# Taking the products of constants out of TensorE's foreseen waits in a four-layer cross-attention kernel

## What is computed

```python
# L0: one-head attention over a projected memory, a gate, an RMS norm
memory_proj = ctx @ W_mem.T;  attn = softmax(x @ memory_proj.T / 16)
c = attn @ memory_proj
x = rmsnorm(x + sigmoid(concat(x, c) @ W_gate.T + b_gate) * c) * norm_w
# L1: 16 heads of 64 over ctx with a mask, then a GELU feed-forward of width 1024
q = layernorm(x) @ Wq;  k, v = split(ctx @ Wkv)
x = x + tanh(attn_gate) * (softmax(mask(q @ k.T / 8)) @ v) @ Wo
x = x + tanh(ff_gate) * gelu(layernorm(x) @ W1) @ W2
# L2, L3: causal self-attention (16 heads of 16, rotary), cross-attention (16 heads of 8),
#         SwiGLU of width 688; two sets of weights, picked per token by the mask vm
x = x + where(vm, a @ v_dense, a @ l_dense)   # a: self-attention of rmsnorm(x)
x = x + cross_attention(rmsnorm(x), ctx) @ cdense_w
x = x + where(vm, ffn_v(rmsnorm(x)), ffn_l(rmsnorm(x)))
```

## Time and profile before

| | us |
|---|---|
| median of 3 runs | 2722.21 (2719.45 to 2730.94) |
| the profiled execution's own time | 2724.13 |
| its span, first to last instruction | 2722.3 |
| TensorE busy in the span | 2627.3 (97%), 19429 matmuls |
| DVE, ACT, POOL busy | 1624.8 (60%), 1318.6 (48%), 974.3 (36%) |

### The profile page before, as it was taken

How to read it: one execution, slowest core, us unless ns; L and a number is a source line. 1 busy time by engine, 2 the same in 40 slices (tenths; PEclk the granted TensorE clock), 3 DMA queues, 4 the chain that set the end, 5 groups by cost and what they waited for, 6 DMA issues and landing times.

```text
span 2722.3 us, 52680 instructions
## 1 busy us (share of the span) xinstructions
PE 2627.3 (97%) x19429; PEld 1584.6 (58%) x19429; DVE 1624.8 (60%) x3532; ACT 1318.6 (48%) x4818; POOL 974.3 (36%) x862
## 2 busy tenths in 40 slices
PE   6999999999999999999999999999999999999998
PEld 4556566665555656566556565656655556566664
DVE  2426567786424547777643454777855345477874
ACT  2446444654343644464444373555534447255452
POOL 0014344553111515555311241654621133155452
PEclk9999999999999999999999999999999999999999
DMA  7000021212201011120220101112121010120111
GB/s 204 1 24 13 21 55 36 52 29 71 67 1 36 2 31 51 30 64 22 70 63 1 35 2 47 43 30 55 29 71 55 1 36 2 51 58 19 48 29 55
DMA packets 171044, 109.52 MB, mean 40 GB/s; under 512 B 31714, under 2 KB 168356, under 8 KB 170660
## 3 DMA queue, kind: packets, MB, share of 16 engines
q1 hardware_dynamic: 166336, 105.82, 14.0%
q10 hardware_dynamic: 4452, 0.29, 0.1%
HBM read 101.87 MB, written 4.19 MB: 39 GB/s over the span
## 4 chain that ended last, share of the span: by engine, by line
PE 81%; DVE 10%; ACT 5%; issue 2%; POOL 1%; ACTq 1%; DVEq 0%
PE bank L1334 11%; PE bank L1351 6%; PE bank L979 5%; PE bank L1057 5%; PE bank L1239 4%; PE bank L1227 4%; PE bank L1248 4%; PE bank L1220 4%; PE bank L1274 3%; ACT Ebuf L1438 3%; PE bank L1340 3%; PE bank L1033 2%; PE bank L1074 2%; PE bank L1211 2%; PE bank L1017 2%
## 5 line engine op out<-in xcount | busy, mean ns | idle before, releaser
L1839 POOL TENSOR_TENSOR Ebuf<-Ebuf,row_rcp 128x512 f32<-128x512 f32 (+1 forms) x328 | 344.4, 1056 | 956.6 <-DVE row_rcp L1655 956.4
L1438 ACT ACTIVATE Ebuf<-bank,minus_max 128x64 f32<-128x64 f32 x1568 | 468.3, 333 | 116.3 <-DVE minus_max L1639 115.4
L1639 DVE TENSOR_REDUCE minus_max<-bank 128x8 f32<-128x512 f32 (+1 forms) x328 | 220.3, 674 | 226.2 <-PE bank L1017 124.5
L1438 ACT ACTIVATION_READ_ACCUMULATOR Ebuf<-bank,minus_max 128x1 f32 x1568 | 353.5, 225 | 0.0
L1447 ACT ACTIVATE PT<-bank 128x512 f32<-128x512 f32 (+1 forms) x328 | 193.7, 603 | 128.2 <-PE bank L1057 125.8
L1057 PE MATMUL bank<-ident,Ebuf 128*128 128x128 f32 x1296 | 200.9, 281 | 10.0 <-POOL Ebuf L1839 9.5
L1057 PEld LDWEIGHTS bank<-ident,Ebuf 128*128 128x128 f32 x1296 | 146.8, 142 | 79.2 <-issue 46.2
L1334 PE MATMUL bank<-xs_b,w_ring 128*128 128x512 f32 (+1 forms) x384 | 170.0, 605 | 2.4 <-DVE xs_b L1733 2.4
L1334 PE MATMUL bank<-xs_a,w_ring 128*128 128x512 f32 (+1 forms) x384 | 168.8, 602 | 0.0
L966 PE MATMUL bank<-causal_bf,ident_bf 128*128 128x512 bf16 x525 | 136.8, 383 | 0.0
L1881 POOL TENSOR_TENSOR arena_b<-arena_b,masks_b 128x384 f32<-128x384 f32 (+1 forms) x48 | 67.7, 1411 | 192.7 <-DVE arena_b L1809 192.6
(11 more groups left out here) (322 smaller groups left out, 5668.8 us busy)
## 6 DMA issues: line engine op xcount, KB each, us to landing
w_ring<-in_L_W SPq DMA_DIRECT2D x64, 256.0 KB, 3.1
w_ring<-in_L_l_gate SPq DMA_DIRECT2D x80, 128.0 KB, 2.2
w_ring<-in_L_l_up SPq DMA_DIRECT2D x80, 128.0 KB, 2.3
w_ring<-in_L_l_down SPq DMA_DIRECT2D x80, 128.0 KB, 2.2
w_ring<-in_L_v_gate SPq DMA_DIRECT2D x80, 128.0 KB, 2.4
w_ring<-in_L_v_up SPq DMA_DIRECT2D x80, 128.0 KB, 2.4
w_ring<-in_L_v_down SPq DMA_DIRECT2D x80, 128.0 KB, 2.5
arena_a<-in_x SPq DMA_DIRECT2D x4, 512.0 KB
```

The costliest lines, as they stand in the source:

```text
L1438: last = A(Ebuf[:, u % UNITS, cell], bank(token)[:, cell], ACT.Exp, bias=minus_max[:, u % UNITS, c:c + 1], accum_out=row_sum[:, u % UNITS, ...
L1639: V.reduce_max(minus_max[:, u % UNITS, 0:g], cells(bank(token)[:, 0:g * S]), AX_X, negate=True).then_inc(maxed, 1)
L1839: G_.tensor_tensor(v, v, row_rcp[:, n % 3, 0:g].unsqueeze(2).broadcast_to([P, g, S]), ALU.mult).then_inc(probs_ready, 1)
```

## The change

The products are taken out, with all that made and counted them. The planner's order, banks and costs and all semaphores remain.

```diff
-FILLER, HOP, SLACK, LEAD, REACH = 0.3, 0.2, 0.1, 10.0, 80.0
+HOP, SLACK, LEAD, REACH = 0.2, 0.1, 10.0, 80.0
...
-    orders, pauses = {engine: [] for engine in clock}, {}
+    orders = {engine: [] for engine in clock}
...
-            return orders, pauses, begin, end, bank_of, held_by
+            return orders, begin, end, bank_of, held_by
...
-            if engine == "PE":
-                pauses[token] = int(max(0.0, at - max(clock["PE"], free)) / FILLER)
...
-ORDER, PAUSES, BEGIN, END, BANK, HELD = schedule(global_order())
-BEFORE_TABLE = set(ORDER["PE"][:ORDER["PE"].index(("table", 0, 0)) + 1])
+ORDER, BEGIN, END, BANK, HELD = schedule(global_order())
...
-            def pause(token, b):
-                if token not in BEFORE_TABLE:
-                    for _ in range(PAUSES[token]):
-                        mm(b[:, :].rearrange("p (h s) -> p h s", h=8), ident_bf[:, :],
-                           causal_bf[:, :].unsqueeze(1).broadcast_to([P, 8, S]), start=True, stop=True)
-
             def fill(token):
                 if HELD[token] is not None:
                     pe.wait_ge(*emptied(HELD[token]))
-                pause(token, bank(token))
                 return bank(token)
```

## The result

The changed kernel takes 2801.98 us (median of 4, 2800.74 to 2806.38) against 2720.83 us for the kernel before on the same chip: ratio 1.030, 95% interval 1.0285 to 1.0316. It is 81 us slower. Its profiled execution has a span of 2798.9 us, 76.6 more than that of before.

The account below looks back on a forecast made before the run. TensorE's own work plus its waits was taken to bound the kernel. From 2724 us, less 12 given back, plus 71 for half clock, came 2783, or 2782 on the median; range 2728 to 2845 us.

Parts of the forecast that it names:

- (a): Line 966's products hold up operands already there; removing them gives back 12 us, bounds 0 and 24.
- (b): Half-clock time once waits are bare: 245 us in all, 212 us beyond the 33 already there.
- six tenths: Share of the 408 us in the thin stretches over four cycles taken to run at half clock: 245 us.
- eight stretches: Places in one cycle, together 102 us, holding 131 products; clock falls were expected in most of them.
- rival 1: Low clock feeds on itself: small-step chains stretch and whole stretches stay low; 2836 to 2845 us, chance 0.16.
- (c): Time lost per us at half clock, from two pairs of twin stretches: 0.335 us, 71 us in all.
- the fall in dense work: From 683.74 to 690.96, 7.22 us against its twin's 5.58: 1.64 us, or 0.48 per us at half clock.
- a clock of 0.955: Sign: mean granted clock of the changed kernel about 0.955, down from 0.994.
- the first dense four: Sign: behind 1337.86, line 1334's first four dense matmuls take about 3.3 us instead of 1.96.
- a cycle of 685 us: Sign: from line 979 at 1131.84 to its twin one cycle later, growing from 670 to about 685 us.
- Rival 2: Products only in the way, clock falls no more: the chain's 24 us come back, 2698 us, chance 0.07.
- Rival 3: Clock falls only where TensorE is truly idle for long, 14 rows at 1.64 us each: 2733 us, chance 0.14.

Follow-up runs that it names:

- e4_no_small: Kernel before, with the products taken out of waits that have only one or two of them (443 remain): 2727.63 us.
- e10_cap4: Kernel before, with at most four products in any wait (362 remain): 2726.1 us.
- e9_quarter: Kernel before, with FILLER 0.25 instead of 0.3, so more products (651 instead of 525): 2719.26 against 2720.13 us.
- e2_thin: Kernel before, with all 525 products still 512 columns wide but over 2 rows of the array instead of 128: 2851.1 us.
- e6_norms: Kernel before, with products only in the waits of norms and projections, none in the attention steps (346 remain): 27.5 us lost.
- e11_cap2: Kernel before, with at most two products in any wait (230 remain): 2750.17 us.
- e1_half: Kernel before, with FILLER 0.6 instead of 0.3, so 229 products, at the head of each foreseen wait: 2738.87 us.
- e12_half_array: Kernel before, with all 525 products at full width but over 64 rows of the array instead of 128: 2761.74 us.

## Why the prediction was right, and by how much its terms were off

The direction, the mechanism (half-clock time in the bared waits outweighs what their removal gives back) and the range held: 2802 us lies in 2728 to 2845, beside a forecast of 2782. By the profiled executions the forecast was a span longer by 59 us (71 less 12), and it is 76.6. The three terms:

**(a) Time given back.** Forecast 12 us, and next to none is seen. The pieces at full clock in both add up to 0.65 us more in the changed kernel, but they hold only about 150 of the 525 products; e4_no_small and e10_cap4, where such pieces hold more of them, show about 2 us. What the rest would give at full clock can't be told apart from the falls. The prediction took half of what the chain of work put on line 966 (its largest piece is 2.77 us at 560.16, not the 2.59 named). Its own check on the largest piece, 0.3 of 2.59 us, was the better reading. Where something was there to be had, it was mostly not kept. The kernel before, then the changed one, TensorE's timeline:

```profile
2082.28 0.66 PE L1057 MATMUL bank<-ident,Ebuf 128*128 128x128 f32 x4
2082.78 0.81 PE L966 MATMUL bank<-causal_bf,ident_bf 128*128 128x512 bf16 x3
2083.42 1.88 PE L1220 MATMUL bank<-xs_a,w_q 128*128 128x512 f32 x4
2085.23 1.15 PE L1074 MATMUL bank<-PT,arena_a 64*64 64x64 f32 x32
...
2090.68 1.88 PE L1227 MATMUL bank<-arena_a,w_o 128*128 128x512 f32 x4
```

```profile
2136.26 0.63 PE L1045 MATMUL bank<-ident,Ebuf 128*128 128x128 f32 x4 [1.30 <-POOL Ebuf L1827]
2136.72 1.88 PE L1208 MATMUL bank<-xs_a,w_q 128*128 128x512 f32 x4
2138.86 1.15 PE L1062 MATMUL bank<-PT,arena_a 64*64 64x64 f32 x32 [0.26 <-issue]
...
2144.38 1.88 PE L1215 MATMUL bank<-arena_a,w_o 128*128 128x512 f32 x4
```

Three products stood before a step whose inputs were there: from line 1057 to line 1220 it took 1.14 us and now 0.46, 0.68 us won. By line 1074 it is 2.60 instead of 2.95: half is gone again, as TensorE now stands idle for 0.26 us (the profile books it as issue; ACT's `PT`, which line 1062 reads, is ready at 2138.77). At line 1227 it is 8.12 against 8.40.

**(b) How much half clock.** Forecast 245 us in all, measured 297. This was the term without a row, and that its six tenths came out near is luck in part. With the two traces laid side by side, the prediction's eight stretches and their twins (29 in all, as the run ends within the fourth cycle) are 434 us long in the changed kernel, and 229 us of them, 0.53, are at half clock. The forecast's shortfall lies outside them: 37 us are where these falls begin before a stretch or run on behind it, and 30 us are elsewhere, 20 of them in the first 90 us of the run. The falls are also longer than the ones of 3.4 and 6.8 us from which the price had been read: there are 29, and 15 of them, of 10.2 to 34.1 us, make up 229 us of the 297 (the equal numbers are chance). That is what rival 1, the low clock that feeds on itself, would look like, but no run shows that a fall prolongs itself; stretches without the products may simply stay thin for longer. The stretch of the earlier trace rows shows a long one. In the changed kernel:

```profile
435.39 1.12 PE L1045 MATMUL bank<-ident,Ebuf 128*128 128x128 f32 x4
...
470.69 1.55 PE L967 MATMUL bank<-xs_a,w_l_qkv 128*128 128x512 f32 x3
```

It takes 35.30 us, against 30.30 with 10.2 us at half clock, and 27.39 at full clock. The 7.91 us lie over 29.2 us of half clock. But not everything stayed low, as that rival's 2836 to 2845 us had it: 229 of the 434 us.

**(c) The price.** Forecast 0.335 us for each us at half clock, measured 76.6/264 = 0.29, and 0.27 in the stretch just shown. I had weighed the fall in dense work, 0.48, with a quarter of the time. That pair of twins was also not quite the same code: between its two ends one ran line 1334 and the other line 1351, in products of the same sizes. Why the long falls cost less is only argued (in small steps part of TensorE's longer time lies beside other engines' work); the stretch just shown agrees. The kernel before gives nearly the same price by itself: of its 23 executions beside e9_quarter, the one with a clock of 0.999 took 2714.61 us, the one with 0.991 took 2727.22. That is 12.6 us for 2 x 0.008 x 2720 = 43.5 us at half clock, or 0.29. These two are the ends; a line through all 23 gives 0.27, and through its 60 executions beside the runs 0.30.

Together: 12 us from (a), (264 - 212) x 0.335 = 17 from (b), and 264 x (0.29 - 0.335) = -12 from (c) make the 17 us between 59 and 76.6. The third offset part of the first two.

What the prediction wanted to see: a clock of 0.955 (0.947), about 3.3 us for the first dense four (3.75), and a cycle of 685 us. The cycle, the changed kernel's line 967 first, then that of before, whose start is in the earlier trace rows:

```profile
1160.12 1.98 PE L967 MATMUL bank<-xs_a,w_l_qkv 128*128 128x512 f32 x4
...
1848.94 1.98 PE L967 MATMUL bank<-xs_a,w_l_qkv 128*128 128x512 f32 x4
```

```profile
1801.55 1.98 PE L979 MATMUL bank<-xs_a,w_l_qkv 128*128 128x512 f32 x4
```

688.8 us against 669.7.

Rival 2 (nothing lost, 24 us back) has neither half: the clock fell, and next to nothing came back. Rival 3, the Trainium skill's rule of idle gaps (TensorE: Matmul & The Clock Gate, section HAM oscillation — how this bites in real kernels), is told of a kernel whose engine really stands between bursts. It is not enough here: in e2_thin the clock falls with the engine busy for 97% and no idle over 1.78 us. That idle can go with a fall the runs do not deny (e10_cap4). The Trainium skill's other statement on that page (section What's actually happening), that activity lifts the throttle, fits if activity is read as use of the array: 128, 64 and 2 rows, all at 525 products, gave 0.994, 0.979 and 0.941.

What stays open: how the spread of products over the waits decides. The runs show that it does (e10_cap4 against e6_norms, e11_cap2 against e1_half), not by what rule. The same thin work can go with a fall in one cycle and without in another: the 32 products at 683.74 have one behind them, their twin at 1357.31 has none. The values of the constants were not varied by themselves, so that rows of the array are what counts rests on e12_half_array, which keeps the constants and halves the rows. How much of the time of e12_half_array is overrun is an estimate and was not tested by itself.

## What to carry to other kernels

Before taking out an engine's idle-time filler, look at the granted clock and ask what would be left in those stretches, in work of the whole array and not in busy time; in e2_thin, busy for 97% with products on 2 rows in the waits, the clock was as low as with none. Filler belongs inside the wait: at most four products in each kept all but 6 of the 81 us here, and filling to the brim cost 10.6 us against before. And time that the chain of work puts on filler was hardly to be had here; look at when the operand was ready.

## What the runs showed of the hardware

- With 525 products in the same waits, each 512 columns wide, the mean clock was 0.994 on 128 rows of the array, 0.979 on 64 and 0.941 on 2, beside 0.947 with no products.
- The clock can stay at half for long with the engine busy: for 34.1 us in the changed kernel, with TensorE busy for 29.98 of them.
- In e2_thin it fell again and again with no idle time over 1.78 us.
- 1 us at half clock cost 0.29 us in this change, 0.30 between 60 executions of the kernel before, and 0.26 to 0.34 in the kernels with fewer products whose clock moved by 0.011 or more.
- The spread of the kernel before, 2714 to 2729 us, goes mostly with its clock, 0.999 to 0.991 (correlation 0.87 over 60 executions between time and half-clock time).
